# Padding scatters spread between the result scatters in a two-layer mixture-of-experts block with attention

## The chip, the cores and the metric

The kernel runs on one core of one Trainium2 chip. The metric is the device time of one execution in microseconds (us); less is better. A core has five engines that each take their own instruction stream in order and meet at semaphores: PE (TensorE, matmuls), DVE (VectorE), ACT (ScalarE), POOL (GpSimd, which here issues the indirect transfers) and SP (SyncE, which here issues the plain transfers).

## The reference

The block is x + FFN/2, then attention, then FFN/2 again, on 4 x 512 tokens of width 256. Only the FFN is touched. It is a mixture of 16 experts with the best 4 for each token:

```
t = xf * jax.lax.rsqrt(jnp.mean(xf * xf, axis=-1, keepdims=True) + EPS) * norm_w
logits = t @ gate_w.T + gate_b
vals, idx = jax.lax.top_k(logits, TOP_K)
gates_k = jax.nn.softmax(vals, axis=-1)
...
h = jnp.einsum('mh,eoh->emo', t, w1) + b1[:, None, :]
a = jnp.minimum(h[..., ::2], LIMIT)
b = jnp.clip(h[..., 1::2], -LIMIT, LIMIT)
act = a * jax.nn.sigmoid(ALPHA * a) * (b + 1.0)
y = jnp.einsum('emi,edi->emd', act, w2) + b2[:, None, :]
delta = jnp.einsum('me,emd->md', G, y)
```

## The kernel before

`moe(m)` is called twice, as m = 0 and m = 1, with `attention()` between. Each call has three stages.

**Routing.** The 2048 tokens are 16 tiles of 128, in four groups g of four tiles. For each group DVE centres the rows, PE turns them and multiplies them with the gate weights, DVE finds the four best experts (`choose`), PE counts by matmuls with a triangle of ones how many earlier tokens chose the same expert (`rank`), and DVE turns these ranks into row numbers (`locate`). Every expert owns a region of REGION rows in the DRAM tensor `x_rows`. POOL scatters the rows of each tile to their four experts, four indirect transfers to a tile, 64 in a stage. `slots()` on DVE then works out the table `slot_tab`: for each of 79 slots its first row in `x_rows`, the place of its goals and its expert. A slot is a tile of 128 rows of one expert, in the experts' order.

**Padding.** An expert's last tile is seldom full. POOL fills it by one scatter of `pad` for each expert, 16 in a stage, 128 rows each, from the row after its last token on. The goal number in a pad row is out of bounds, so that its result is dropped. Slot n < 16 belongs to an expert not above n, so SP waits before loading the rows of slot n for pads up to that of expert n. Before the change the pads count on five semaphores, for experts 0, 1, 2 to 3, 4 to 7 and 8 to 15 (`PADS`), and SP waits at slots 0, 1, 2, 4 and 8.

**Slots.** For n = 0 to 78 SP reads two numbers of slot n from `slot_tab` (`value_load`, two of them), issues the load of its rows and that of its goals into one of NX = 8 buffers (`load_rows`), PE turns the rows (`turn_rows`), ACT copies them to SBUF (`rows_out`), PE does the first product (`up`), ACT and DVE the gelu and the clipping, PE turns h (`turn_h`), does the second product (`down`), ACT copies y to SBUF (`y_out`), and POOL scatters y to the DRAM tensor `y_rows`. For n of 8 and more, SP's load waits until PE has turned slot n - 7 and until y of slot n - 8 is stored. PE goes in iterations s: up(s), turn_rows(s + 2), turn_h(s - 1), down(s - 2). ACT goes gelu(s), rows_out(s + 2), h_hi(s), y_out(s - 2). Neither has another order to fall back on: what stands behind a waiting instruction waits too.

At the end DVE adds the four results of each token (`combine`).

Of the kernel before, what the change touches and what calls it, by code (L numbers as in the profile page):

```python
# [19 lines left out]
ALU = mybir.AluOpType  # L20
# [25 lines left out]
def build(nc, x, wqkv, bias_qk, bv, wo, bo, query_rows, key_rows, norm_w, gate_w, gate_b, w1, b1, w2, b2, out):  # L46
# [56 lines left out]
    with ctx:  # L103
# [26 lines left out]
        def moe(m):  # L130
            with ExitStack() as own:
# [34 lines left out]
                pos = tmp("pos", [P, TPB, E])  # L166
                row_to = tmp("row_to", [P, NT, K], u32)
# [31 lines left out]
                PADS = (1, 2, 4, 8, 16)  # L199
                padded = [ev(f"padded{j}") for j in range(len(PADS))]  # L200
                pad_group = lambda e: next(j for j, last in enumerate(PADS) if e < last)

# [6 lines left out]
                with nc.Block() as block:  # L209
                    @block.sync  # L210
                    def _(sp):
# [6 lines left out]
                        def load_rows(n):  # L218
                            c = n % NX
                            row0 = sp.value_load(slot_tab[0:1, 0, n:n + 1], min_val=0, max_val=E * REGION + (E - 2) * P)  # L220
                            cell = sp.value_load(slot_tab[0:1, 1, n:n + 1], min_val=0,  # L221
                                                 max_val=(E * REGION + (E - 2) * P + 1) * ROW - 1)
                            if n >= NX:
                                sp.wait_ge(ev("turned"), n - NX + 1)
                                sp.wait_ge(y_stored[(n - NX) % NY], (n - NX) // NY * 16 + 16)
                            if n < E and n in (0,) + PADS:
                                sp.wait_ge(padded[pad_group(n)], 16 * (PADS[pad_group(n)] - n))
                            sp.dma_start(rows[:, c, :], x_rows[m].bitcast(f16)[bass.ds(row0, P), 0:2 * H]).then_inc(loaded[c], 16)
                            cells = x_rows[m].rearrange("r c -> (r c)")
                            sp.dma_start(goal[:, c, :], cells[bass.ds(cell, P * ROW)]  # L230
                                         .rearrange("(p c) -> p c", p=P)[:, 0:1],
                                         allow_slow_non_contiguous=True).then_inc(loaded[c], 16)
# [26 lines left out]
                        sp.wait_ge(ev("slot_tab"), 1)  # L259
                        sp.wait_ge(ev("idle_made"), 16)  # L260
                        for c in range(NR):
                            sp.wait_ge(scattered[c], NT // NR * K * 16)
                        for n in range(SLOTS):
                            load_rows(n)
# [14 lines left out]
                    def _(pool):  # L279
# [35 lines left out]
                        for e in range(E):  # L315
                            pool.indirect_dma_start(x_rows[m], bass.IndirectOffsetOnAxis(ap=pad_at[:, e:e + 1], axis=0),
                                                    pad[:, :], None).then_inc(padded[pad_group(e)], 16)
                        for n in range(SLOTS):
                            c = n % NX
                            pool.wait_ge(loaded[c], 32 * (n // NX) + 32)  # L320
                            pool.wait_ge(ev("y"), n + 1)
                            pool.indirect_dma_start(y_rows[m], bass.IndirectOffsetOnAxis(ap=goal[:, c, :], axis=0),  # L322
                                                    y[:, n % NY, :], None, bounds_check=K * T - 1, oob_is_err=False).then_inc(y_stored[n % NY], 16)

                    @block.tensor
                    def _(pe):
# [18 lines left out]
                        def rank(g):  # L345
# [6 lines left out]
                            for i in range(g * TPB):  # L352
                                pe.matmul(bank[4][:, 0:TPB * E].rearrange("p (t e) -> p t e", e=E), ones16[:, :],
                                          mask16[:, i:i + 1, :].broadcast_to([P, TPB, E]), start=False, stop=False,
                                          skip_group_check=True)
# [7 lines left out]
                            for t in range(TPB):  # L363
                                i = g * TPB + t
                                mm = pe.matmul(bank[5][:, 0:E], ones16[:, :], mask16[:, i, :], start=(i == 0),
                                               stop=(i == NT - 1), skip_group_check=True)
                            if g == B - 1:
                                mm.then_inc(ev("counts"), 1)
# [86 lines left out]
                    def _(act):  # L455
# [34 lines left out]
                        for g in range(B):  # L490
# [22 lines left out]
                            if m == 0:  # L513
                                for _ in range(SPLITS[g]):
                                    hi_split(split)
                                    split += 1
                        rows_out(0)
# [15 lines left out]
                    def _(dve):  # L533
# [87 lines left out]
                        def locate(g):  # L621
# [3 lines left out]
                                              region[:, :].unsqueeze(1).broadcast_to([P, TPB, E]), ALU.add)\  # L625
# [4 lines left out]
                            with nc.allow_low_precision("whole numbers"):  # L630
                                dve.tensor_reduce(row_to[:, some, :], work[:, :, :, :], AX.X, ALU.add)\  # L631
                                   .then_inc(ev("row_to"), 1)

# [9 lines left out]
                        def slots():  # L643
                            dve.wait_ge(ev("counts"), 1)
                            step(dve.tensor_scalar(count[:, :], bank[5][:, 0:E], P - 1.0, None, ALU.add))
                            dve.scalar_tensor_tensor(pad_at[:, :], bank[5][:, 0:E], place[:, 0:1], region[:, :],
                                                     ALU.add, ALU.add).then_inc(ev("pad_at"), 1)
# [72 lines left out]
                        if m == 0:  # L720
                            dve.wait_ge(ev("constants"), 9)
                        for g in range(B):
# [590 lines left out]
```

## Time and profile before

| what | value |
|---|---|
| median of 3 runs | 1123.13 us (1119.69 to 1123.15) |
| the profiled execution | 1121.11 us |
| its span | 1119.4 us |
| mean granted TensorE clock | 0.863 of full |
| PE busy | 737.8 us (66%) |
| DVE busy | 622.3 us (56%) |
| ACT busy | 425.2 us (38%) |
| POOL busy | 370.7 us (33%) |

The span is the time from the first to the last instruction; 1.7 us of the execution lie outside it. A busy share is an average over stages with different limits, so the stages are read apart. In what follows, m0 and m1 are the two calls, and all times without another word are from the start of the span.

### The profile page before, as it was taken

Reading aid. Unit: us, or ns where it says so; the run is one execution under the profiler, and the core shown is the slowest. Engines: PE = TensorE matmul, PEld = TensorE weight load, DVE = VectorE, ACT = ScalarE, POOL = GpSimd, SP = SyncE. Lnnn points to the kernel's source line nnn. Section 1 sums busy time; section 2 is a strip of 40 time slices with the busy share of each in tenths; the row PEclk is TensorE's granted clock in tenths of the full one; section 3 lists DMA queues with packets and bytes.
Section 4 is the critical chain, followed back from the end, with each engine's and each line's share of the span. In section 5 each row is a group of like instructions: output and inputs, shape, how many; then the busy total and the mean of one; then the engine's idle time right before and its main releaser. Section 6 shows DMA issues by size and latency. Waiting matters only on the chain. (4 is left out here: it accounts for less than half of the span.)

```text
span 1119.4 us, 22068 instructions
## 1 busy us (share of the span) xinstructions
PE 737.8 (66%) x5770; PEld 449.6 (40%) x5770; DVE 622.3 (56%) x1953; ACT 425.2 (38%) x945; POOL 370.7 (33%) x404
## 2 busy tenths in 40 slices
PE   2222169999999107658999998531205999999930
PEld 1112036666666003323343443421202666666620
DVE  6876036566665484446767672462502656665537
ACT  3433035555555012204545454110103555555510
POOL 4866723333333103440000000064772333333320
PEclk9999989999999657866999999755556999999975
DMA  9752323333332553420111100222232333333347
GB/s 321 253 211 94 118 75 91 87 96 89 91 88 83 188 169 95 131 76 16 45 31 35 33 27 3 76 87 72 98 113 72 92 93 96 94 93 92 83 146 230
DMA packets 110387, 114.31 MB, mean 102 GB/s; under 512 B 38836, under 2 KB 96669, under 8 KB 110272
## 3 DMA queue, kind: packets, MB, share of 16 engines
q1 hardware_dynamic: 95008, 73.82, 23.1%
q0 software_dynamic: 15264, 39.10, 9.4%
q8 instruction: 55, 0.90, 0.3%
q14 instruction: 60, 0.49, 0.1%
HBM read 60.89 MB, written 55.56 MB: 104 GB/s over the span
## 5 line engine op out<-in xcount | busy, mean ns | idle before, releaser
L322 POOL DMA_INDIRECT y_rows<-y_m,goal_m x158 | 155.6, 985 | 302.2 <-ACT y_m L486 282.9
L394 PE MATMUL banks<-w1s,rT_m 128*128 x948 | 234.6, 384 | 0.0
L671 DVE TENSOR_SCALAR b_m<-banks 128x256 f32<-128x256 f32 x158 | 67.1, 425 | 218.2 <-ACT p_m L472 110.3
L312 POOL DMA_INDIRECT x_rows<-row_m,row_to_m x128 | 135.0, 1054 | 121.2 <-DVE row_to_m L631 83.7
L1197 DVE CUSTOM_DVE_ANT_0 junk<-banks,maskq 128x128 bf16<-128x128 f32 (+3 forms) x256 | 115.6, 488 | 44.9 <-PE banks L1046 41.8
L465 ACT ACTIVATE rT_m<-banks 128x512 f16<-128x512 f16 x158 | 93.5, 592 | 105.4 <-issue 78.3
L394 PEld LDWEIGHTS banks<-w1s,rT_m 128*128 128x128 f16 x948 | 93.9, 99 | 97.5 <-issue 5.0
L416 PE MATMUL banks<-w2s,hT_m 128*128 x948 | 129.2, 273 | 0.0
L1166 ACT ACTIVATE probs<-banks 128x1024 f32<-128x1024 f32 (+3 forms) x128 | 86.1, 703 | 88.7 <-PE banks L1082 88.5
L376 PE MATMUL banks<-ident,rows_m 128*128 128x128 f16 x632 | 62.7, 223 | 79.2 <-DMA goal_m<-x_rows 40.0
L472 ACT ACTIVATE p_m<-banks 128x256 f32<-128x256 f32 x158 | 60.7, 384 | 116.7 <-PE banks L394 111.2
L376 PEld LDWEIGHTS banks<-ident,rows_m 128*128 128x128 f16 x632 | 48.9, 100 | 119.0 <-DMA goal_m<-x_rows 43.1
L416 PEld LDWEIGHTS banks<-w2s,hT_m 128*128 128x128 f16 x948 | 92.6, 98 | 8.9
L479 ACT ACTIVATE hs_m<-h_m 128x256 f16<-128x256 f32 x158 | 65.8, 417 | 73.8 <-DVE h_m L679 45.1
L1046 PE MATMUL banks<-k_stack,q_stack 63*128 63x128 f16 (+3 forms) x256 | 72.0, 327 | 21.9 <-DVE mx L1197 9.7
L686 DVE TENSOR_TENSOR hs_m<-h_m,hs_m 128x256 f16<-128x256 f32 x158 | 67.2, 426 | 30.6 <-ACT hs_m L479 7.8
L332 PE MATMUL banks<-ident,u_m 128*128 128x128 f32 x64 | 19.8, 436 | 82.3 <-DVE u_m L576 52.9
L679 DVE SCALAR_TENSOR_TENSOR h_m<-p_m,b_m 128x256 f32<-128x256 f32 x158 | 67.1, 425 | 5.4
L709 DVE SCALAR_TENSOR_TENSOR X<-arena_m,gate_m,X 128x256 f32<-128x256 f32 x128 | 51.4, 477 | 31.3 <-DMA arena_m<-y_rows 30.9
L1002 POOL COPY v_near<-v 128x272 f32<-128x272 f32 x16 | 6.6, 416 | 182.7 <-PE banks L1095 182.7
L693 DVE COPY hT_m<-banks 128x512 f16<-128x512 f16 x158 | 65.8, 416 | 1.0 <-PE banks L403 1.0
L403 PE MATMUL banks<-ident,hs_m 128*128 128x128 f16 x632 | 61.3, 220 | 4.1 <-DVE hs_m L686 2.6
(165 smaller groups left out, 1160.4 us busy)
## 6 DMA issues: line engine op xcount, KB each, us to landing
rows_m<-x_rows SPq DMA_DIRECT2D x158, 128.0 KB
arena_m<-y_rows SPq DMA_DIRECT2D x32, 512.0 KB, 5.4
arena_m<-in_w SPq DMA_DIRECT2D x16, 512.0 KB, 7.4
arena_m<-in_w SPq DMA_DIRECT2D x16, 256.0 KB, 8.4
qk_split<-w_raw SPq DMA_DIRECT2D x32, 128.0 KB
x_rows<-pad SPq DMA_DIRECT2D x2, 2040.0 KB, 9.9
q_stack<-qk_split SPq DMA_DIRECT2D x32, 96.0 KB
k_stack<-qk_split SPq DMA_DIRECT2D x32, 96.0 KB
```

The source lines that it names most:

```text
L312: pool.indirect_dma_start(x_rows[m], bass.IndirectOffsetOnAxis(ap=row_to[:, i, k:k + 1], axis=0), row[:, i % NR, :], None).then_inc(scatte ...
L322: pool.indirect_dma_start(y_rows[m], bass.IndirectOffsetOnAxis(ap=goal[:, c, :], axis=0), y[:, n % NY, :], None, bounds_check=K * T - 1, o ...
L376: mm = pe.transpose(bank16[n % 2][:, q * P:(q + 1) * P], rows[:, c, q * P:(q + 1) * P], ident16[:, :])
L394: mm = pe.matmul(o, rT[:, n % 2, 2 * r + k, :], w1s[:, bass.ds(e, 1), k, w, :], start=False, stop=(k == HC - 1 and w == 1))
L416: mm = pe.matmul(o, hT[:, n % 2, 2 * r + k, :], w2s[:, bass.ds(e, 1), k, w, :], start=False, stop=(k == 1 and w == 1))
L465: act.activation(rT[:, n % 2], bank16[n % 2][:, 0:512].rearrange("p (q n) -> p q n", q=4), ACT.Copy).then_inc(ev("rT"), 1)
L671: dve.tensor_scalar(b[:, n % 2, :], bank[2 + n % 2][:, INNER:], (LIMIT + 1.0) * S, (1.0 - LIMIT) * S, ALU.min, ALU.max).then_inc(ev("b"), 1)
L679: dve.scalar_tensor_tensor(h[:, n % 2, :], p[:, n % 2, :], GELU_LIMIT, b[:, n % 2, :], ALU.min, ALU.mult).then_inc(ev("h"), 1)
L686: dve.tensor_tensor(hs[:, n % 2, 2:4, :], h[:, n % 2, :].rearrange("p (k n) -> p k n", k=2), hs[:, n % 2, 0:2, :], ALU.subtract).then_inc( ...
L1046: pe.matmul(bank[u % 2][:, 0:(i + 1) * P], stacks[0][at:at + HALF - 1, pair, i * P:(i + 1) * P], stacks[1][at:at + HALF - 1, pair, 0:(i + ...
L1166: act.activation(probs[j][:, 2 * pl:2 * pl + 2, :], banks[:, first:first + 2, 0:SEQ - j * P], ACT.Exp, scale=0.25).then_inc(s("exp"), 1)
L1197: dve.tensor_tensor_reduce(junk[:, (n * U + u) % 3, 0:W], bank[u % 2][:, 0:W], maskq[:, SEQ - W:], 1.0, -3e38, ALU.add, ALU.max, mx[:, n % ...
```

## The change

The diff, cut to its core:

```
-                PADS = (1, 2, 4, 8, 16)
-                padded = [ev(f"padded{j}") for j in range(len(PADS))]
-                pad_group = lambda e: next(j for j, last in enumerate(PADS) if e < last)
+                padded = [ev(f"padded{e}") for e in range(E)]
+                AHEAD = 6
...
-                        def load_rows(n):
-                            c = n % NX
+                        def place_of(n):
                             row0 = sp.value_load(slot_tab[0:1, 0, n:n + 1], ...)
                             cell = sp.value_load(slot_tab[0:1, 1, n:n + 1], ...)
+                            return row0, cell
+
+                        def load_rows(n, row0, cell):
+                            c = n % NX
...
-                            if n < E and n in (0,) + PADS:
-                                sp.wait_ge(padded[pad_group(n)], 16 * (PADS[pad_group(n)] - n))
+                            if n < E:
+                                sp.wait_ge(padded[n], 16)
...
                         sp.wait_ge(ev("slot_tab"), 1)
+                        places = [place_of(n) for n in range(4)]
                         sp.wait_ge(ev("idle_made"), 16)
...
                         for n in range(SLOTS):
-                            load_rows(n)
+                            load_rows(n, *(places[n] if n < 4 else place_of(n)))
...
-                        for e in range(E):
+                        def pad_expert(e):
                             pool.indirect_dma_start(x_rows[m], ... pad_at[:, e:e + 1] ...,
-                                                    pad[:, :], None).then_inc(padded[pad_group(e)], 16)
+                                                    pad[:, :], None).then_inc(padded[e], 16)
+
+                        for e in range(AHEAD):
+                            pad_expert(e)
                         for n in range(SLOTS):
                             c = n % NX
+                            if 1 <= n and n - 1 + AHEAD < E:
+                                pad_expert(n - 1 + AHEAD)
                             pool.wait_ge(loaded[c], 32 * (n // NX) + 32)
                             pool.wait_ge(ev("y"), n + 1)
...
-                            for i in range(g * TPB):
-                                pe.matmul(bank[4][:, 0:TPB * E]..., ones16[:, :], mask16[:, i:i + 1, :]...)
...
-                                mm = pe.matmul(bank[5][:, 0:E], ones16[:, :], mask16[:, i, :], start=(i == 0), ...)
-                            if g == B - 1:
-                                mm.then_inc(ev("counts"), 1)
+                                mm = pe.matmul(bank[5][:, g * E:(g + 1) * E], ones16[:, :], mask16[:, i, :], start=(t == 0), ...)
+                            mm.then_inc(ev("counts"), 1)
...
+                        act.preload_act_table_set("gelu_apprx_sigmoid_and_others")
                         rows_out(0)
...
-                                              region[:, :].unsqueeze(1).broadcast_to([P, TPB, E]), ALU.add)\
+                                              base[:, g, :].unsqueeze(1).broadcast_to([P, TPB, E]), ALU.add)\
...
+                            dve.wait_ge(ev("counts"), g + 1)
+                            step(dve.tensor_tensor(base[:, g + 1, :], base[:, g, :], bank[5][:, g * E:(g + 1) * E], ALU.add))
```

Four things change. (1) Only the pads of experts 0 to 5 follow the row scatters; that of expert n + 5 now stands just ahead of the scatter of y of slot n, for n = 1 to 10, and every one of slots 0 to 15 has a wait for its own pad. (2) SP reads the places of slots 0 to 3 before it waits for the row scatters. (3) `rank` no longer multiplies the masks of all earlier groups; DVE carries the totals in `base` and adds the group's counts after each group. (4) ACT loads the table of the gelu before rows_out(0), not at the first gelu.

POOL's instructions at the end of routing in m0, before (what an instruction waits for stands in brackets; `y_0` is the semaphore of y_out in m0):

```order
L312 DMA x_rows<-row_m,row_to_m 36992x272 [waits row_to_0,row_hi_0]
L312 DMA x_rows<-row_m,row_to_m 36992x272 x3
L316 DMA x_rows<-pad,pad_at_m 36992x272 [waits pad_at_0]
L316 DMA x_rows<-pad,pad_at_m 36992x272 x15
L322 DMA y_rows<-y_m,goal_m 8192x256 [waits y_0,rows_loaded0_0]
L322 DMA y_rows<-y_m,goal_m 8192x256 [waits y_0,rows_loaded1_0]
```

and of the changed kernel at the same place, L320 the pads and L331 the scatters of y:

```order
L316 DMA x_rows<-row_m,row_to_m 36992x272 x3
L320 DMA x_rows<-pad,pad_at_m 36992x272 [waits pad_at_0]
L320 DMA x_rows<-pad,pad_at_m 36992x272 x5
L331 DMA y_rows<-y_m,goal_m 8192x256 [waits y_0,rows_loaded0_0]
L320 DMA x_rows<-pad,pad_at_m 36992x272
L331 DMA y_rows<-y_m,goal_m 8192x256 [waits y_0,rows_loaded1_0]
```

Ten pads have moved behind a scatter that waits for y, the pad of expert 6 behind that of slot 0, and so on one by one.

SP's instructions for slot 2 in m0, before:

```order
L220 TENSOR_LOAD slot_tab_m
L220 ISA x2
L221 TENSOR_LOAD slot_tab_m
L221 ISA x2
L228 ISA [waits padded2_0]
L228 DMA rows_m<-x_rows 128x512
L230 REGISTER_ALU
L230 DMA goal_m<-x_rows 128x1
```

and of the changed kernel, for slot 2, slot 3 and slot 6's wait:

```order
L231 ISA [waits padded2_0]
L231 DMA rows_m<-x_rows 128x512
L233 REGISTER_ALU
L233 DMA goal_m<-x_rows 128x1
L231 ISA [waits padded3_0]
L231 DMA rows_m<-x_rows 128x512
L233 REGISTER_ALU
L233 DMA goal_m<-x_rows 128x1
...
L231 ISA [waits padded6_0]
```

The reads of the table are gone from between the first four loads, and slots 3, 5, 6 and so on, which had no wait for a pad, have one.

## Rows read from the trace of the kernel before

**Rows 1.** Busy time by stretch: start:end, length, busy of each engine, PEclk, DMA.

```profile
125.00:154.00 29.00, 8.06 (x29) 3.40 (x30) 1.27 (x3) 3.81 (x7) 14.71 (x16) 0.84 0.31 100
826.00:857.00 31.00, 4.49 (x20) 2.29 (x21) 0.00 (x0) 2.73 (x4) 15.66 (x17) 0.50 0.26 90
857.00:1075.00 218.00, 214.83 (x1721) 141.83 (x1718) 132.55 (x332) 123.06 (x314) 75.81 (x77) 1.00 0.31 86
```

**Rows 2.** Timeline, end of routing in m0: start, length, engine, line, operation.

```profile
137.15 0.61 PE L376 MATMUL banks<-ident,rows_m 128*128 128x128 f16 x4 [6.29 <-issue]
...
143.31 0.97 POOL L316 DMA_INDIRECT x_rows<-pad,pad_at_m  x1 [0.30 <-issue]
...
147.85 0.00 SPq L228 DMA_DIRECT2D rows_m<-x_rows  x1
...
149.88 0.61 PE L376 MATMUL banks<-ident,rows_m 128*128 128x128 f16 x4 [9.14 <-DMA goal_m<-x_rows]
```

**Rows 3.** Timeline of POOL in m1: the first and the last pad.

```profile
826.42 0.97 POOL L316 DMA_INDIRECT x_rows<-pad,pad_at_m  x1 [0.30 <-issue]
...
845.57 0.97 POOL L316 DMA_INDIRECT x_rows<-pad,pad_at_m  x1 [0.30 <-issue]
```

**Rows 4.** Chain of waits in m1, from the last row scatter to slot 1.

```profile
827.67 0.70 SPq L220
...
833.03 0.70 SPq L228
...
851.23 0.00 SPq L228
...
851.93 1.14 DMA goal_m<-x_rows
```

**Rows 5.** Timeline in m1: turns of slots 1, 4, 6; scatters of y 0 to 2.

```profile
853.12 0.61 PE L376 MATMUL banks<-ident,rows_m 128*128 128x128 f16 x4 [13.55 <-DMA goal_m<-x_rows]
...
860.95 0.39 PE L376 MATMUL banks<-ident,rows_m 128*128 128x128 f16 x4
...
866.69 0.39 PE L376 MATMUL banks<-ident,rows_m 128*128 128x128 f16 x4
...
864.04 1.00 POOL L322 DMA_INDIRECT y_rows<-y_m,goal_m  x1 [17.50 <-ACT y_m L486]
867.04 0.99 POOL L322 DMA_INDIRECT y_rows<-y_m,goal_m  x1 [2.01 <-ACT y_m L486]
869.75 0.98 POOL L322 DMA_INDIRECT y_rows<-y_m,goal_m  x1 [1.71 <-ACT y_m L486]
```

**Rows 6.** Chain of waits: transfers that ended a wait, from their issue to landing.

```profile
804.73 2.45 DMA x_rows<-row_m,row_to_m
...
896.96 4.12 DMA y_rows<-y_m,goal_m
...
909.16 4.10 DMA goal_m<-x_rows
...
1076.52 2.11 DMA y_rows<-y_m,goal_m
```

**Rows 7.** Timeline of ACT in m1: h_hi in a steady iteration.

```profile
868.22 0.42 ACT L479 ACTIVATE hs_m<-h_m 128x256 f16<-128x256 f32 x1 [0.46 <-issue]
```

**Rows 8.** Timeline of PE in m1: the first product of slot 0 and of slot 3.

```profile
853.95 2.77 PE L394 MATMUL banks<-w1s,rT_m 128*128 x6
...
862.67 1.46 PE L394 MATMUL banks<-w1s,rT_m 128*128 x6
```

**Rows 9.** Timeline of ACT in m1: table load and first gelu.

```profile
854.38 1.28 ACT L472 ACT_TABLE_LOAD   x1
...
856.75 0.39 ACT L472 ACTIVATE p_m<-banks 128x256 f32<-128x256 f32 x1 [1.09 <-PE banks L394]
```

**Rows 10.** Timeline in m0, group 3: ranks, row numbers, the scatters behind them.

```profile
94.78 0.83 PE L353 MATMUL banks<-mask_m,ones 128*128 128x64 f16 x12
...
99.99 0.22 DVE L624 TENSOR_TENSOR pos_m<-banks,region 128x64 f32<-128x64 f32 x1 [5.16 <-remote]
...
101.91 0.97 POOL L312 DMA_INDIRECT x_rows<-row_m,row_to_m  x1 [3.94 <-DVE row_to_m L631]
```

More of the change, by code:

```diff
@@ L166, in moe @@
                 pos = tmp("pos", [P, TPB, E])
+                base = tmp("base", [P, B + 1, E])
                 row_to = tmp("row_to", [P, NT, K], u32)
@@ L351, in rank @@
                                       skip_group_check=True)
-                            for i in range(g * TPB):
-                                pe.matmul(bank[4][:, 0:TPB * E].rearrange("p (t e) -> p t e", e=E), ones16[:, :],
-                                          mask16[:, i:i + 1, :].broadcast_to([P, TPB, E]), start=False, stop=False,
-                                          skip_group_check=True)
                             for t in range(TPB - 1):
@@ L364, in rank @@
                                 i = g * TPB + t
-                                mm = pe.matmul(bank[5][:, 0:E], ones16[:, :], mask16[:, i, :], start=(i == 0),
-                                               stop=(i == NT - 1), skip_group_check=True)
-                            if g == B - 1:
-                                mm.then_inc(ev("counts"), 1)
+                                mm = pe.matmul(bank[5][:, g * E:(g + 1) * E], ones16[:, :], mask16[:, i, :], start=(t == 0),
+                                               stop=(t == TPB - 1), skip_group_check=True)
+                            mm.then_inc(ev("counts"), 1)
                         def turn_rows(n):
@@ L643, in slots @@
                         def slots():
[L644 to L647, printed above, removed]
+                            step(dve.scalar_tensor_tensor(count[:, :], base[:, B, :], P - 1.0, region[:, :],
+                                                          ALU.add, ALU.subtract))
+                            dve.tensor_scalar(pad_at[:, :], base[:, B, :], place[:, 0:1], None, ALU.add)\
+                               .then_inc(ev("pad_at"), 1)
                             step(dve.tensor_scalar(count[:, :], count[:, :], 7, None, ALU.arith_shift_right))
@@ L721, in _ @@
                             dve.wait_ge(ev("constants"), 9)
+                        step(dve.tensor_copy(base[:, 0, :], region[:, :]))
                         for g in range(B):
```

## The prediction, made before the changed kernel ran

> **What bounds the kernel now.** I read the table of stages first. The slot stages are near full use of PE: 214.83 us busy in 218 us, at the full clock of 2.4 GHz. Between routing and slots there is a hole: from 826 to 857 us PE works 4.49 us, in m0 from 125 to 154 us 8.06 us, while POOL is busy half the time [rows 1]. The change works on these two holes and on the first slots behind them.
>
> The timelines show what fills the holes. POOL's pads run without a pause, 0.97 us and a gap of 0.30 us each, so one every 1.28 us, from 826.42 to 846.5 us in m1 [rows 3] and up to 144.3 us in m0 [rows 2]. They are not what SP waits for: a row scatter takes 2.45 us from its issue to landing [rows 6], so the pad of expert 1, which slot 1 needs, lands at about 830.2 us. The chain of waits shows SP itself crawling, its register steps and reads of the table in steps of 0.70 us, from 827.67 to 851.23 us [rows 4]. It gets fast 4.7 us after POOL's last pad has ended. In m0 the load of slot 2 goes out at 147.85 us, 3.6 us after the last pad [rows 2]. So in both calls a long unbroken run of POOL's scatters goes with a slow SP, which recovers about 4 us after the run. What the one does to the other the trace doesn't say. I take the end of the run as what sets the end of the hole.
>
> **What the change takes away.** Ten pads leave the run: 10 x 1.28 = 12.8 us. SP then gets fast at about 851.2 - 12.8 = 838.4 us in m1. PE turned slot 1 1.9 us after SP's load of it (851.23 to 853.12 us, [rows 4, 5]), so now at about 840.4 us. The early reads help to have this: in the slow stretch reading the table for slot 0 took from 827.67 to 833.03 us, 5.4 us [rows 4], and for slots 1 to 3 the reads are now done while the last row scatters run. Slots 0 and 1 are thus loaded by the time that SP is fast, and the gain in m1 is the whole 12.7 us. In m0 slot 1 was turned already at 137.15 us, and what came late was slot 2, at 149.88 us [rows 2]. Here SP gets fast at 135.1 us, slot 2 follows at about 138, behind slot 1 and the first product: a gain near 12 us. Sum of both: **24.5 us**. The bounds are 20 us (SP recovers some 2 us later in each call than I take) and 36.5 us (the slow stretch is gone: slot 1 in m1 at 830.2 + 2.3 = 832.5, 20.5 us early, and slot 2 in m0 at 134, 16 us early).
>
> **What the change puts on the path.** The pad of expert n, for n = 6 to 15, is issued behind the scatter of y of slot n - 6, and SP waits for it before it loads slot n. In the trace of before, y of slot 0 is scattered at 864.04 us and PE turns slot 6 at 866.69 us, 2.65 us later [rows 5]; for slot 7 it is 867.04 and 866.69 + 2.72 = 869.41, so 2.37 us. (2.72 us is the period of a slot: the scatters of y at 867.04 and 869.75 us stand 2.71 us apart.) All of this would be moved early together. In that distance the changed kernel must fit a path L of three terms:
>
> - The pad is issued 1.28 us behind the scatter of y [rows 3].
> - It lands: 2.45 us for a row scatter of the same size, 2.11 us for the last scatter of y, alone, and 4.12 us for one amid the slots' traffic [rows 6]. I take 2.8 us, nearer to the lone ones, since POOL and SP now take turns.
> - SP issues the load of rows and goals, and they land: 1.9 us from the load to PE's turn in m1, 2.0 us in m0 [rows 2, 4, 5], and 4.1 us for the goals alone amid traffic [rows 6]. I take 2.7 us, because the next scatter of y and its pad fall into this load.
>
> L = 1.28 + 2.8 + 2.7 = 6.8 us; at the least 1.28 + 2.11 + 1.9 = 5.3, at the most 1.28 + 4.12 + 4.2 = 9.6 us. Even the least is twice the 2.65 us that are there, so PE waits.
>
> It waits again and again, because the loop closes on itself. Behind PE's turn of slot n stands, in PE's order, down(n - 4), and behind ACT's copy of slot n stand h_hi and y_out of the same iteration. The turn of slot 4 at 860.95 and y of slot 0 at 864.04 are 3.09 us apart [rows 5]. In a stall h is ready before, so that ACT's idle 0.46 us ahead of h_hi falls away [rows 7], and 2.6 us are left. So slot n + 2 can be turned no sooner than 2.6 + L after slot n, where before two slots took 5.44 us. With L = 6.8 that is 9.4 us for two slots. Slots 6 to 15 are five pairs. The first loses L - 2.37, the others L + 2.6 - 5.44 = L - 2.84 each: 5 L - 13.7 in all, **20.3 us** in a call and **40.6 us** in both. The bounds are 12.8 and 34.3 us in a call. From slot 16 on there is no pad to wait for. Scatters of y are then eight slots ahead of the loads as before, and PE takes up its period at once. What was lost isn't given back, since PE has next to nothing free there [rows 1].
>
> The waits for pads 0 to 5 cost nothing: they are issued by 834 us, in the stretch in which SP is slow anyway.
>
> **Ranks.** PE drops 4, 8 and 12 matmuls in groups 1 to 3; twelve take 0.83 us. In m0, group 3, the path from ranks to POOL is bare: POOL stands idle 3.94 us for row_to, and DVE before it 5.16 us for the ranks [rows 10]. I take group 2, with eight matmuls, to be alike. DVE gains one small addition a group (0.22 us, as that of L624), behind row_to, and once the wait for `counts`. I count a gain of 0.6 + 0.8 - 0.4 = **1 us** in m0 and none in m1, where POOL has 16 scatters of the group before to go through. If DVE's 5.16 us were the matmuls themselves, up to 6 us could come back, if the extra waits were slow in the slow stretch as SP's steps were, 2 us lost.
>
> **Table of the gelu.** The load takes 1.28 us from 854.38 us, and the first gelu starts at 856.75, just when the product that it waits for ends (853.95 + 2.77 = 856.72) [rows 8, 9]. It is hidden by the product, so moving it early brings nothing. Without that cover it would cost the 1.28 us. The Trainium skill ("ScalarE: Activation LUTs", What ACT_TABLE_LOAD costs) has about 2.66 us for a switch, a drain of 1.38 us included; were this on the path, the sum would be 5.3 us lower. The row shows it under the product, and I keep zero.
>
> **Sum.** 1121.1 (the profiled execution) - 24.5 + 40.6 - 1 = 1136.2 us. The profiled execution is 2.0 us under the median of the three runs, so I put the forecast at **1137 us**, 14 us or 1.2% slower.
>
> **The rivals.**
> *The burst wins (faster).* The same two terms, the other way: if the slow stretch vanishes with the shorter run (36.5 us gained) and L is near its least, 5.4 us (13.3 us lost in a call), the result is 1121.1 - 36.5 + 26.6 - 1 = 1110 us. It turns at 5 L - 13.7 = 12.3 us in a call, L = 5.2 us, with the gain that I take, and at L = 6.4 us with the full gain. For it speaks that SP's slowness has no cause in its own work, and that row scatters also run ahead of it, at the same pace; against it that these, 16 to a group, stay in the run, and SP was slow at 827.67 us, before a second pad could matter.
>
> *A wash.* The two terms within 3 us of each other, for instance L = 5.8 us with a gain of 30: 1121.1 - 30 + 30.6 - 1, so 1121 us. It is what is left between.
>
> *The clock falls in the stalls.* PE would stand still some 4 us of each 9.4. Over the hole of m0 the granted clock is 0.84 on the mean, so it fell to the lower level while PE stood idle, and in that of m1 it stood at 0.50 throughout [rows 1]: six matmuls of the first product took 2.77 us at 1.2 GHz and 1.46 us at 2.4 GHz [rows 8]. If it falls in the stalls, turn_h and the second product between a turn and y take about 1 us longer, once for each pair, in 10 pairs: 10 us, and 1147 us. The Trainium skill ("TensorE: Matmul & The Clock Gate", Part 1) has the clock set by how busy PE has lately been, which speaks for it; at 60% busy in the stalled slots I think it mostly holds.
>
> *The waits don't bind*, because the pads come in time: excluded by the 2.65 us of [rows 5], which are less than the landing of one transfer and its load.
>
> **Chances and range.** My forecast 0.60 (its own range 1126 to 1150 us), the clock's fall on top 0.14, a wash 0.11, the burst wins 0.15. The range of 8 in 10 goes from 1116 to 1160 us: the lower end takes in the wash, the upper one L = 8.5 us or the clock with L = 7.5 us. A difference under 0.3% (3.4 us) is no change for this measurement. Faster 0.15, same 0.11, slower 0.74.
>
> **What would show it.** In the changed profile the last of the six pads starts at about 7.7 us behind the last row scatter, in both calls. SP's first four loads stand close together, and slot 1 is turned some 12 us sooner after the last row scatter in m1. From slot 6 to 15 PE's turns wait for loads of goals or rows, in pairs 9 to 10 us apart, and the chain of waits runs over y, POOL, x_rows, goal and PE; from slot 16 the period is 2.72 us. ACT's table load stands before the first rT. I am wrong if pads land so fast that the pairs are under 8 us apart, if SP is quick at once, or if SP stays slow through the new pattern of two scatters for a slot.

## The result, and the profile after

The changed kernel takes **1149.56 us** (median of 4 runs, 1147.31 to 1151.09), the kernel before in the same rounds 1123.14 us (1119.69 to 1124.46). The ratio is 1.0231, its 95% interval 1.0199 to 1.0263: 26 us slower, where 14 were forecast. The time lies in the range of 1116 to 1160 us, and at the upper edge of the forecast's own range. The profiled execution has a span of 1145.6 us against 1119.4.

The page of the changed kernel, its busy time and the group of PE's turns of the rows (a turn is the transposition of a slot's rows by PE, `turn_rows`):

```profile
PE 752.8 (66%) x5722; PEld 451.5 (39%) x5722; DVE 624.8 (55%) x1963; ACT 426.1 (37%) x945; POOL 368.4 (32%) x404
...
L380 PE MATMUL banks<-ident,rows_m 128*128 128x128 f16 x632 | 63.6, 225 | 72.4 <-DMA goal_m<-x_rows 72.4
```

Nearly all of PE's idle time ahead of its turns is put down to loads of goals. PE does fewer matmuls than before and is busy longer, which points to a lower clock. The table of stages tells where (start:end, length, busy of PE, its weight loads, DVE, ACT and POOL, then clock, DMA share and GB/s):

```profile
125.00:154.00 29.00, 17.35 (x104) 9.59 (x105) 7.71 (x19) 8.67 (x20) 6.86 (x7) 0.97 0.26 75
144.00:196.00 52.00, 35.73 (x217) 20.17 (x215) 16.09 (x40) 16.02 (x40) 20.05 (x20) 0.84 0.25 76
...
836.00:865.00 29.00, 11.66 (x69) 6.33 (x70) 4.49 (x11) 5.54 (x13) 7.04 (x9) 0.61 0.22 67
865.00:916.00 51.00, 36.02 (x222) 19.78 (x219) 16.93 (x42) 16.61 (x42) 20.58 (x21) 0.87 0.26 81
916.00:1100.00 184.00, 181.70 (x1451) 120.36 (x1451) 111.18 (x279) 102.48 (x263) 64.93 (x66) 0.99 0.31 86
```

The holes of [rows 1] are partly filled: from 125 to 154 us PE is busy 17.35 us, where it was busy 8.06. Behind them stands what was not there before, some 50 us in each call in which PE is busy 70% of the time, at a granted clock of 0.84 and 0.87. Behind slot 16 PE is as busy as before: 181.70 us of 184 from 916 us on, where [rows 1] have 214.83 of 218.

The timeline of m0 shows one round of the new stall and the last of the six pads (start, length, engine, line, operation, and in brackets the idle time ahead and what ended it):

```profile
127.67 0.97 POOL L320 DMA_INDIRECT x_rows<-pad,pad_at_m  x1 [0.30 <-issue]
...
144.38 0.99 POOL L331 DMA_INDIRECT y_rows<-y_m,goal_m  x1 [15.73 <-ACT y_m L490]
145.68 0.99 POOL L320 DMA_INDIRECT x_rows<-pad,pad_at_m  x1 [0.30 <-issue]
148.32 0.33 SPq L231 DMA_DIRECT2D rows_m<-x_rows  x1
150.69 0.40 PE L380 MATMUL banks<-ident,rows_m 128*128 128x128 f16 x4 [3.49 <-DMA goal_m<-x_rows]
...
153.04 2.75 PE L398 MATMUL banks<-w1s,rT_m 128*128 x6
154.09 1.00 POOL L331 DMA_INDIRECT y_rows<-y_m,goal_m  x1 [4.43 <-ACT y_m L490]
155.40 0.98 POOL L320 DMA_INDIRECT x_rows<-pad,pad_at_m  x1 [0.30 <-issue]
155.60 0.41 PE L380 MATMUL banks<-ident,rows_m 128*128 128x128 f16 x4
```

Y of slot 0 goes out at 144.38, the pad of expert 6 at 145.68, SP's load of slot 6 at 148.32, and PE turns it at 150.69 us: 6.31 us, the forecast's L. The turn of slot 7, at 155.60 us, has no idle time ahead: it stands right behind the first product of slot 5, which began at 153.04 us and took 2.75 us. The chain of waits in m1 shows a whole turn of the loop (start, length, what):

```profile
869.21 1.78 DMA goal_m<-x_rows
870.99 0.05 issue
871.04 0.40 PE banks L380 x4
871.43 0.36 issue
871.79 0.38 PE banks L407 x4
872.18 0.11 PE banks L416
872.28 1.02 PE banks L420 x6
873.31 0.02 issue
873.33 0.39 ACT y_m L490
...
873.84 0.73 issue
874.57 0.99 POOL y_rows L331
875.56 0.30 issue
875.87 2.69 DMA x_rows<-pad,pad_at_m
...
878.77 0.33 SPq L231
...
879.28 1.44 DMA goal_m<-x_rows
880.72 0.33 issue
881.05 0.40 PE banks L380 x4
```

From turn to y 3.53 us, from y to the turn two slots on 6.48 us, together 10.0 us for two slots, which took 5.44 before [rows 5]. What SP waited for from 864 to 916 us (us in all, times, the longest) is nearly all pads:

```profile
SPq L230 <- DMA x_rows<-pad,pad_at_m: 24.1, 8, 4.9
```

**Where the 26.2 us went.** I cut each call at the last row scatter and at PE's turns of slots 5 and 15.

| stretch | before m0, m1 | after m0, m1 | change |
|---|---|---|---|
| start to last row scatter, m0 | 122.90 | 120.03 | -2.9 |
| last row scatter to turn of slot 5 | 36.1, 38.8 | 24.3, 28.4 | -22.2 |
| turn of slot 5 to turn of slot 15 | 27.2, 27.2 | 53.4, 50.8 | +49.8 |
| all the rest | | | +1.5 |

Of the rest, 2.2 us lie at slot 16 of m1, which is turned 4.94 us after slot 15 and not 2.72, behind a first product of 2.53 us. The next turn comes 2.72 us later.

### The profile page after: what moved, and what is told of

The parts are those of the page before. It is cut to its first block and busy times, and to the rows that moved or that the text cites. A ratio compares the mean times of both kernels' runs of the same rounds, so it can differ in the third digit from the quotient of the medians.

```text
span 1145.6 us, 21990 instructions
## 1 busy us (share of the span) xinstructions
PE 752.8 (66%) x5722; PEld 451.5 (39%) x5722; DVE 624.8 (55%) x1963; ACT 426.1 (37%) x945; POOL 368.4 (32%) x404
## 3 DMA queue, kind: packets, MB, share of 16 engines
q1 hardware_dynamic: 95008, 73.82, 22.5%
## 5 line engine op out<-in xcount | busy, mean ns | idle before, releaser
L331 POOL DMA_INDIRECT y_rows<-y_m,goal_m x158 | 155.7, 985 | 329.4 <-ACT y_m L490 305.6
L398 PE MATMUL banks<-w1s,rT_m 128*128 x948 | 243.2, 395 | 0.0
L316 POOL DMA_INDIRECT x_rows<-row_m,row_to_m x128 | 132.1, 1032 | 121.6 <-DVE row_to_m L636 84.1
L1205 DVE CUSTOM_DVE_ANT_0 junk<-banks,maskq 128x128 bf16<-128x128 f32 (+3 forms) x256 | 115.6, 488 | 44.7 <-PE banks L1054 41.7
L398 PEld LDWEIGHTS banks<-w1s,rT_m 128*128 128x128 f16 x948 | 96.2, 101 | 104.1 <-issue 16.0
L420 PE MATMUL banks<-w2s,hT_m 128*128 x948 | 133.0, 278 | 0.0
L407 PE MATMUL banks<-ident,hs_m 128*128 128x128 f16 x632 | 61.5, 220 | 8.0 <-issue 4.9
```

The costliest lines, as they stand in the source:

```text
L398: mm = pe.matmul(o, rT[:, n % 2, 2 * r + k, :], w1s[:, bass.ds(e, 1), k, w, :], start=False, stop=(k == HC - 1 and w == 1))
L407: mm = pe.transpose(bank16[4 + n % 2][:, q * P:(q + 1) * P], hs[:, n % 2, q, :], ident16[:, :])
L420: mm = pe.matmul(o, hT[:, n % 2, 2 * r + k, :], w2s[:, bass.ds(e, 1), k, w, :], start=False, stop=(k == 1 and w == 1))
L1205: dve.tensor_tensor_reduce(junk[:, (n * U + u) % 3, 0:W], bank[u % 2][:, 0:W], maskq[:, SEQ - W:], 1.0, -3e38, ALU.add, ALU.max, mx[:, n % ...
```

## The experiments

Their ratios stand against the kernel before in the same rounds; its median moved from 1120.61 to 1124.56 us between the sets of rounds, so where two experiments come from different sets I compare ratios. In the diffs, lines with - are the changed kernel's. Times "after the last row scatter" run from its start to PE's turn of a slot, m0 and m1.

### How many pads go first

`e1_all_pads_first`: the change without its new order, all 16 pads behind the row scatters.

```
-                AHEAD = 6
+                AHEAD = 16
```

> The changed kernel with AHEAD = 16, so that all pads follow the row scatters again; ranks, early reads, table and one semaphore for each pad stay. Theory W (SP's waits for pads issued behind y cost 24 us in m0 and 26 us in m1, the shorter run of scatters gives 10.4 us in each call back): 1149.6 - 49.8 + 20.8 = 1120.6 us, 2.5 us under the kernel before, all of it from routing in m0. Rival T (the waits of SP for one pad each, or the other three edits, cost the time): near 1149 us.

`e2_ahead_10`, `e3_ahead_8` and later `e10_ahead_7`: the same line with 10, 8 and 7.

> AHEAD = 10: six pads go behind scatters of y, but each ten slots ahead. Between the scatter of y of slot n - 10 and the turn of slot n lie 2.65 + 4 x 2.72 = 13.5 us, twice the path L of 6.3 to 6.8 us. Theory W: no stall, and six pads at 1.04 us each less in the run: 1120.6 - 12.5 = 1108 us. Rival T (two scatters in a slot's time crowd POOL or the DMA engines): six slots a call with 2.5 us lost each, so 1108 + 30 = 1138 us.

> AHEAD = 8: eight pads go behind scatters of y, each eight slots ahead: 2.65 + 2 x 2.72 = 8.1 us are there, L was 6.3 to 6.8 us. Theory W: it just fits, and the run is eight pads shorter: 1120.6 - 16.6 = 1104 us, the fastest. If L is over 8.1 us amid full traffic (4.1 us for landing and 3.5 us for the load were seen there), stalls of 1 us for a slot come back and it ends near 1115 us. Rival T: near 1144 us.

> The changed kernel with AHEAD = 7. The loop then closes over three slots: the turn of slot n + 3 comes no sooner than 3.4 + L = 9.8 us after that of slot n (L = 6.4 as measured with AHEAD = 6), where three slots take 8.16 us: 0.55 us a slot for nine slots, 5 to 6 us a call, against 24 to 26 with AHEAD = 6. By that the time lies halfway between AHEAD = 6 (1149.6) and 8 (1117.4), but nearer to 8: 1117.4 + 11 + 2 = 1130 us. If the loss were by traffic of pad and y together, one place more would change nothing: 1148 us.

| pads first | median us | ratio, interval | slot 2, us after last row scatter | slot 5 to slot 15, us | SP's waits for pads there, us |
|---|---|---|---|---|---|
| 6 (the change) | 1149.56 | 1.0231, 1.0199 to 1.0263 | 16.6, 20.9 | 53.4, 50.8 | 26.0, 25.0 |
| 7 | 1122.39 | 0.9988, 0.9958 to 1.0018 | 22.4, 22.5 | 38.1, 37.0 | 8.6, 7.1 |
| 8 | 1117.39 | 0.9934, 0.9901 to 0.9967 | 23.1, 23.5 | 33.8, 34.5 | 2.3, 2.8 |
| 10 | 1116.82 | 0.9950, 0.9923 to 0.9978 | 25.6, 26.0 | 30.5, 32.9 | none |
| 16 | 1125.61 | 1.0007, 0.9981 to 1.0033 | 33.2, 34.4 | 27.2, 27.2 | none |

(Pairs are m0 and m1. The fifth column runs from PE's turn of slot 5 to that of slot 15, as in the table of the stretches.)

With 16 first the loss is gone, so it belongs to the moved pads. From 16 to 10 and 8 slot 2 comes 8 to 11 us sooner in each call, where 1.28 us a pad would give 7.7 and 10.2; from 16 to 6 it comes 16.6 and 13.5 us sooner, for 12.8. So the shorter run does what was forecast of it; at 10 and 8 it wins.

Between 7 and 6 lie 27 us. The loop takes 10.0 us, from the turn of slot n over y of slot n - 4 and its pad to the turn of slot n + 2 with 6 pads first, of n + 3 with 7, of n + 4 with 8, and two, three and four slots have 5.4, 8.2 and 10.9 us at their period of 2.72: a deficit of 4.6, of 1.8 and none. I expected 1130 us of 7 and got 1122.39: the direction held, the size not.

That is not all that the moved pads cost. From slot 5 to slot 15 the deficit of 1.8 us in three slots makes 6 us in a call, and the turns lose 10.9 and 9.8; with 8 pads first it makes nothing, and they lose 6.6 and 7.3; with 10, 3.2 and 5.7. At 10 SP waits for no pad in that stretch, so this isn't the loop of the pads. It is most of why 10 and 8 missed what was expected of them without a stall, 1108 and 1104 us; the rest came with e1, itself 5 us over its 1120.6, for which see the early reads. What SP waits for there is the landing of y (of slot n - 8 before it loads slot n), with 10 pads first in m1:

```profile
SPq L230 <- DMA y_rows<-y_m,goal_m: 8.1, 4, 3.1
```

With 16 first it waits for the same, but 4.5 us in six times, and the turns keep their pace. The likely cause is the one that e4 shows below: a scatter between two scatters of y costs time by itself. By which way these waits reach PE no run separates. The scan has its flat bottom from 8 to 10.

### The pads alone, and the table alone

`e9_pads_alone`: the kernel before, with the new order of the pads (AHEAD = 6) and their 16 semaphores and nothing else of the change.

```
 (the kernel before)
+                        for e in range(AHEAD):
+                            pad_expert(e)
                         for n in range(SLOTS):
+                            if 1 <= n and n - 1 + AHEAD < E:
+                                pad_expert(n - 1 + AHEAD)
```

> The kernel before with the pads' edit alone: AHEAD = 6, a semaphore for each pad, the pads of experts 6 to 15 behind scatters of y. If the pads carry the whole loss: the changed kernel's 1149.6 us, plus 3 us for the ranks that are missing, minus 2 to 4 us for the early reads that are missing: 1147 to 1151 us. If the other edits share in it: nearer to 1140 us.

1151.62 us (1145.05 to 1155.31), ratio 1.0230 (1.0180 to 1.0280). The pads alone carry the whole loss. Its trace has the same parts: slot 5 to slot 15 takes 51.3 and 53.5 us, 50.4 us more than before in both calls, and slot 5 is turned 24.7 and 27.8 us after the last row scatter. The rest of the change as made adds up to nothing that this measures, to within some 5 us; it may hold a gain and a loss that cancel.

`e8_table_alone`: the kernel before with the one line that loads the gelu's table early.

```
+                        act.preload_act_table_set("gelu_apprx_sigmoid_and_others")
                         rows_out(0)
```

> The kernel before with only the table of the gelu loaded ahead of rows_out(0). If the load is hidden by the first product, as the profile showed: 1124 us, no change (within 0.2%). If it was on the path, by its 1.28 us in both calls, 2.6 us (0.23%) less, by the skill's 2.66 us a switch 5.3 us less.

1122.32 us, ratio 1.0007 (0.9986 to 1.0028): no change. In the changed kernel the load stands in ACT's idle time (timeline of ACT, m0):

```profile
99.85 1.28 ACT L521 ACT_TABLE_LOAD   x1
```

### Is it the waiting or the traffic?

`e4_spare_scatters`: as e1, with a scatter of `pad` to a tensor that nobody reads ahead of the scatters of y of slots 1 to 10, where the change has its pads. Nothing waits for them but the end of the call; the extra tensor, its indices and these twenty scatters are added work.

```
-                AHEAD = 6
+                AHEAD = 16
...
-                            if 1 <= n and n - 1 + AHEAD < E:
-                                pad_expert(n - 1 + AHEAD)
+                            if 1 <= n <= 10:
+                                pool.indirect_dma_start(spare_rows[m], ..., pad[:, :], None).then_inc(ev("spare_done"), 16)
```

> All 16 pads follow the row scatters as in the kernel before; and in the places of the ten moved pads POOL issues ten scatters of the same size and data to a spare tensor that nobody reads, so the output is whole and only work is added. It has the traffic and POOL's order of the changed kernel without SP's wait. Theory W: as with all pads first, 1120.6 us, at most 3 us more. Rival T (traffic, POOL's time): 1120.6 + 49.8 = 1170 us.

1136.96 us, ratio 1.0111 (1.0077 to 1.0144), 11.4 us over e1 in the same rounds. The turns keep their 2.7 us up to slot 7; then PE stalls in places, from slots 8 and 9 on, the first whose loads wait for y of eight slots before. From slot 5 to slot 15 SP's waits for such landings come to 7.5 and 10.2 us, where e1 has 6.7 and 4.5. From the turn of slot 2 to that of slot 15 it takes 41.7 and 44.5 us in m0 and m1, where e1 has 34.2 and 34.9: 17 us more, some 7 us of it made up by a shorter hole in this profiled execution. So 128 more rows to scatter between two y are not free, 0.57 us each by the times and 0.86 by these turns. I had put them at nothing, at most 3 us. This bounds the traffic's part in the change from above only loosely, since here they are extra work, while the change moves its pads.

### The early reads

`e5_all_first_late_reads` is e1, `e6_ahead_8_late_reads` is e3, both with the places of slots 0 to 3 read as before the change, each ahead of its own load.

```
-                        places = [place_of(n) for n in range(4)]
...
-                            load_rows(n, *(places[n] if n < 4 else place_of(n)))
+                            load_rows(n, *place_of(n))
```

> All pads first (AHEAD = 16) and the places of slots 0 to 3 read at their slots as in the kernel before; of the change only the ranks on carried totals, the early table and one semaphore a pad are left. Theory R (the early reads cost time in the slow stretch: SP must step through eight reads at 0.7 us a step before it issues slot 0's load): slot 2 is turned 27 and 31 us after the last row scatter as before, against 33.2 and 34.4 us with the early reads, and the time is 1125.6 - 7 = 1118 us, 0.2 to 0.5% under the kernel before by the earlier routing. Rival (early reads do no harm): 1125 us.

> AHEAD = 8 with late reads. Theory R: slot 0 is turned in the slow stretch, 14 us after the last row scatter, slot 1 some 2 us after SP gets fast, so about 2 us earlier in each call than with early reads: 1117.4 - 4 = 1113 us. Rival (early reads help, since SP has less to do once it is fast): 1120 us.

e5: 1117.39 us, ratio 0.9969 (0.9950 to 0.9988), where e1 has 1.0007. e6: 1111.62 us, 0.9920 (0.9890 to 0.9950), where e3 has 0.9934. By the ratios the late reads are better by 4 us with all 16 pads first, just clear of the uncertainty, and by 1.6 us with 8, which is within it. The traces show the mechanism. SP and PE in m0, of e1 (timeline, one fence), from the last pad on:

```profile
140.45 0.97 POOL L320 DMA_INDIRECT x_rows<-pad,pad_at_m  x1 [0.30 <-issue]
...
146.66 0.36 SPq L231 DMA_DIRECT2D rows_m<-x_rows  x1
...
149.06 0.61 PE L380 MATMUL banks<-ident,rows_m 128*128 128x128 f16 x4 [30.87 <-DMA goal_m<-x_rows]
```

and of e5, timeline of the same place:

```profile
126.92 0.71 SPq L231 DMA_DIRECT2D rows_m<-x_rows  x1
...
130.27 0.61 PE L379 MATMUL banks<-ident,rows_m 128*128 128x128 f16 x4 [14.39 <-issue]
...
139.07 0.97 POOL L319 DMA_INDIRECT x_rows<-pad,pad_at_m  x1 [0.30 <-issue]
```

With two reads ahead of it the first load goes out at 126.92 us, amid the run, and slot 0 is turned 11.6 us after the last row scatter, where it is 29.0 with eight. By slot 5 only 2.8 us are left of that lead. The eight reads do crawl under the run, as the chain of waits of the changed kernel shows in m1:

```profile
845.23 0.69 SPq L220
...
848.73 0.69 SPq L220
...
850.41 0.36 SPq L231
```

There slot 0 is turned 16.5 us after the last row scatter, at 852.81 us, where it was 13.8 us before the change. It is not so in every call: in m0 of the changed kernel and of e4, which has e1's early reads and its 16 pads, the first load goes out at 128.00 and 130.48 us. Whether the eight reads are done before the slow stretch begins seems to decide it. With six pads first the reads made no difference that the traces show: e9, which reads late, has slot 5 at 24.7 and 27.8 us after the last row scatter, the changed kernel at 24.3 and 28.4.

### Breaking the run of scatters

`e7_gate`: late reads, six pads, then POOL waits for the rows of slot 3 to be loaded, then four more pads, and the other six one by one as in e2.

```
-                AHEAD = 6
+                AHEAD = 10
...
-                        for e in range(AHEAD):
+                        for e in range(6):
+                            pad_expert(e)
+                        pool.wait_ge(loaded[3], 32)
+                        for e in range(6, AHEAD):
                             pad_expert(e)
```

> Six pads follow the row scatters, then POOL waits until slot 3's rows are loaded, then pads 6 to 9 follow, and from there AHEAD = 10; late reads. Theory S (SP is slow because POOL's scatters run without a pause, and gets fast 4 to 5 us after a pause begins): SP gets fast as in the changed kernel, slot 2 is turned 17 to 21 us after the last row scatter instead of 26, pads 6 to 9 land well before slot 6: 1116.8 - 10 = 1107 us. Rival (SP's slowness depends on the number of pads or on time since the table was made): no gain over AHEAD = 10, 1117 us. Pad 6 is issued at slot 3's load, 3 slots or 8 us ahead of the turn of slot 6; if that is too late, 2 us are lost in each call.

1106.80 us (1105.30 to 1108.33), ratio 0.9869 (0.9841 to 0.9897): the lowest median of this study, 14 us under before. Its timeline in m0:

```profile
126.61 0.97 POOL L319 DMA_INDIRECT x_rows<-pad,pad_at_m  x1 [0.30 <-issue]
...
126.68 0.70 SPq L231 DMA_DIRECT2D rows_m<-x_rows  x1
131.33 0.33 SPq L231 DMA_DIRECT2D rows_m<-x_rows  x1
...
138.70 0.97 POOL L319 DMA_INDIRECT x_rows<-pad,pad_at_m  x1 [11.13 <-DMA goal_m<-x_rows]
```

SP's load takes 0.70 us while POOL scatters and 0.33 us 3.8 us after the sixth pad has ended (127.58). Slot 2 is turned 17.8 and 20.0 us after the last row scatter, as in the changed kernel, and pads 6 to 9 are there early enough: slot 15 comes after 57.7 and 61.5 us, where the changed kernel needs 77.7 and 79.2. Against e2 this kernel has two things changed, the gate and the late reads. The nearest kernel without the gate is e6 of the same rounds, late reads and 8 pads first: 1111.62 us, none of its runs (from 1110.20) as low as the highest of this one (1108.33). So the gate is worth some 5 us over the best kernel without it; 10 pads first with late reads and no gate was not run.

`e11_gate_after_4`: the same with the gate behind four pads, at the rows of slot 1.

```
-                        for e in range(6):
+                        for e in range(4):
                             pad_expert(e)
-                        pool.wait_ge(loaded[3], 32)
-                        for e in range(6, AHEAD):
+                        pool.wait_ge(loaded[1], 32)
+                        for e in range(4, AHEAD):
```

> As the kernel with the gate (1106.8 us), but only four pads follow the row scatters, POOL then waits for slot 1's rows, and pads 4 to 9 follow. Theory S: the first run is 2.6 us shorter in each call and SP gets fast that much sooner: 1106.8 - 5 = 1102 us. The second run of six pads is 7.7 us; if it makes SP slow again while slots 2 to 5 are loaded, the gain is lost or turned round: 1107 us or more.

1107.44 us (1102.46 to 1113.31), ratio 0.9856 (0.9806 to 0.9906), the same as e7. Slot 2 comes 2.5 and 2.2 us sooner still, after 15.3 and 17.8 us, and the six pads behind the gate take it back, so that the 1102 us of a shorter first run did not come. Timeline in m0:

```profile
132.99 0.97 POOL L319 DMA_INDIRECT x_rows<-pad,pad_at_m  x1 [6.12 <-DMA goal_m<-x_rows]
...
135.85 0.33 SPq L233 DMA_DIRECT2D goal_m<-x_rows  x1
...
139.39 0.70 SPq L231 DMA_DIRECT2D rows_m<-x_rows  x1
141.52 0.01 SPq L233 DMA_DIRECT2D goal_m<-x_rows  x1
```

SP's step is 0.33 us at 135.85 and 0.70 us again at 139.39, 6.4 us into the second run of pads, and the load of the goals follows 2.1 us behind that of the rows, as in the slow stretch. Slot 5 is turned after 26.3 us in m0, where e7 has 24.9.

## Why the prediction was right or wrong, point by point

The forecast's own change was +15.1 us of the profiled execution, and the spans differ by 26.2. The 11.1 us between them are 9.2 of the loop, 2.3 of the holes and 1.5 of the rest, less 1.9 that routing in m0 was shorter than forecast. (1136.2 us and the 2.0 us that the profiled execution lies under the median make 1138 and not 1137 us.)

**The loop of pads: right in kind, 9 us too small.** Two slots take 10.7 us in m0 and 10.2 in m1 from slot 5 to slot 15, and behind them the period of 2.72 us is back (turns at 200.41 and 203.13 us). e9 shows that these pads alone make the whole loss, e1 that it is gone with them. The odd slots from 5 to 15 form a chain without a gap, from each turn to the y of four slots before and from that to the turn of two slots on. Five distances from turn to y, and five from y to turn, which is L:

| | forecast, each call | m0 | m1 |
|---|---|---|---|
| turn to y, each | 3.07, then 2.6 | 3.07, 3.10, 4.26, 3.22, 3.11 | 3.07, 3.07, 3.41, 3.12, 3.82 |
| sum | 13.5 | 16.8 | 16.5 |
| L, each | 6.8 | 8.21, 7.79, 6.25, 6.67, 7.69 | 8.20, 6.82, 6.57, 6.51, 6.21 |
| sum | 34.0 | 36.6 | 34.3 |

The term that was mis-sized most is "2.6 us are left" from a turn to y: 6.3 of the 9.2 us by which 49.8 exceeds 40.6. No turn of this stretch has its y sooner than 3.07 us, the distance of the steady state, so ACT's idle 0.46 us did not fall away; that is 3.8 us in eight distances. The other 2.5 us are restarts. Most of it stands in the two longest distances, 4.26 and 3.82 us: turn_h begins up to 0.4 us after the turn has ended, and the second product takes 1.48 and 1.46 us where it takes 0.82 in the steady state (timeline), at a granted clock of 0.50 (166.50 to 169.60 us) and 0.52 (906.50 to 908.00 us). L makes the other 2.9 us. The rounds shown above are among its shorter ones, 6.31 and 6.48 us: issue 1.3, from the pad to the load of the rows 2.6 and 2.9 (2.8 taken for the landing), load to turn 2.4 and 2.3 (2.7 taken). The longest stand at slot 7 in both calls, 8.2 us, and there PE did not wait for the load: the turn stands behind a first product of 2.75 and 2.62 us, where the steady state has 1.46.

**The clock: a rival that came partly true.** It was given as another way, with 10 us on top. PE's rows in the first restart of m0 (windows, columns as above):

```profile
150.60:154.00 3.40, 2.95 (x19) 1.79 (x20) 0.76 (x2) 1.28 (x3) 0.00 (x0) 0.74 0.16 39
154.00:155.50 1.50, 1.50 (x5) 0.48 (x4) 0.00 (x0) 0.00 (x0) 1.10 (x2) 0.50 0.00 0
```

PE had stood idle 3.49 us, and the granted clock is 0.74 and then 0.50, which is 1.2 GHz; the first product at 153.04 us takes 2.75 us, as it did in [rows 8] at that clock. "At 60% busy in the stalled slots I think it mostly holds" was wrong: it fell in stalls, though not through all of them (0.84 on the mean). What the engine did before the fall agrees with the Trainium skill ("TensorE: Matmul & The Clock Gate", Part 1), by which the clock follows how busy PE has lately been. How much of the 9 us is the clock and how much the restart itself no run separates. An estimate from rows: the 2.5 us of the restarts between turn and y and the 1.4 us by which L exceeds 6.8 at slot 7 of each call stand beside such slow products, some 5 us of the 9.2.

**The traffic of the moved pads: not in the sum.** e4 shows that such scatters between y cost time by themselves, 0.57 us each by their times. In the changed kernel it lies inside the measured distances. In the two rounds shown, landing and load were not longer than forecast; slot 9 of m0 was turned 3.84 us after its load went out (162.65 to 166.49 us), for 2.7 taken. With 8 and 10 pads first, where the loop hardly binds, it is the likely cause of what is left of the loss.

**The gain in the holes: right in kind, 22.2 us for 24.5.** The last of six pads starts 7.64 us behind the last row scatter in m0 and 7.66 in m1, as forecast. By slot 5 m0 has gained 11.8 us, for 12 forecast, and m1 10.4, for 12.7. SP gets fast 5.2 us after POOL's run in m1 (844.93 to 850.12), where 4.7 was taken, and slot 1 is turned 17.5 us after the last row scatter, for 15.3 forecast. "Slots 0 and 1 are thus loaded by the time that SP is fast" did not happen: the first load of m1 goes out at 850.41 us. "The early reads help to have this" was wrong as well: in m1 they put the load of slot 0 behind eight slow reads in place of two, and it comes later. But this isn't what the missing 2.3 us are made of, since e9 without the early reads has the same gain, 22.5 us; there slot 1 is turned 17.0 us after the last row scatter, its own reads still to come when SP gets fast. With all 16 pads first the early reads do cost time (e1 against e5).

**Ranks: 2.9 us in these two traces, where 1 was taken.** DVE's wait in group 3 [rows 10] fell from 5.16 to 0.19 us (timeline of DVE, m0):

```profile
96.06 0.22 DVE L629 TENSOR_TENSOR pos_m<-banks,base_m 128x64 f32<-128x64 f32 x1 [0.19 <-issue]
...
102.50 0.17 DVE L639 TENSOR_TENSOR base_m<-base_m,banks 128x16 f32<-128x16 f32 x1 [5.30 <-issue]
```

The wait has moved to the new addition, behind row_to and off POOL's path. How much that is worth the traces don't fix. The last row scatter of m0 starts at 122.90, 121.23 and 128.77 us in the three traces without the new ranks (before, e8, e9) and at 118.63 to 121.73 us in the ten with them, so 2.9 us is within what one kernel and the next differ by. By the times, e5 is the nearest to the ranks alone (with them only the table, which does nothing, and one semaphore for each pad): ratio 0.9969, 1 to 6 us gained, between the 1 us taken and the 6 named as the upper bound. In m1 nothing came of it, as forecast (93.56 us from first to last row scatter before, 93.70 after).

**The table: hidden, as forecast.** e8 shows it. The 2.66 us that the Trainium skill ("ScalarE: Activation LUTs", What ACT_TABLE_LOAD costs) gives for a switch would have been 5.3 us in two calls; the run shows none of it, since [rows 8, 9] had it under a product.

**The burst wins, and the wash,** have fallen for six pads: L was 6.9 us on the mean of the 20 slots, and the slow stretch did not vanish. With 8 pads first the time does fall, 7 us under before in e3, by way of a longer lead and not of a quick SP. That the time came inside the forecast's own range owes something to its width, 24 us.

**What stays open** is why SP crawls while POOL issues scatters back to back. In e7 it ended 3.8 us after a pause of POOL began, and in e11 a second run brought it back within 6.4 us; what of POOL's run does it (its instruction stream, descriptors or packets) no run separates. Open too is how a scatter between two y stalls PE. e6 against e3 is too near to its uncertainty to size the reads at eight pads.

## What to carry to other kernels

A transfer that stands in order behind work of the pipeline's own output must be ahead of its reader by more slots than the loop takes: add issue, landing, load, and the way from the reader back to that output, and divide by the period. Here 10 us by 2.72 is 3.7 slots, and the pads had two; the lead of 7 and 8 bought back what the loop took, until the longer run cost as much. Take the way back whole, with the order of the instructions on each engine and at the speed of a restart, and take nothing off for idle time in it that no trace shows to go. Scatters put between the result scatters cost something even where nothing waits for them. And if one engine slows while another issues a long run, a wait that breaks the run at the point where the first data are in can be worth more than a shorter run, while work moved early into the slow stretch delays what stands behind it.

## What the runs showed of the hardware that I had not expected

- SP's steps of 0.70 us come and go with POOL's unbroken runs of scatters: in e7 back to 0.33 us at 131.33, 3.8 us after a run, in e11 back to 0.70 us 6.4 us into a second one.
- One pad more ahead, 7 for 6, was worth 27 us: 1122.39 against 1149.56 us.
- From the same reads and 16 pads first, the first load of m0 went out 26.6 us after the last row scatter in e1 and 8.8 us after it in e4 (146.66 and 130.48 us).
- Twenty scatters of 128 rows that nothing in the slots waits for cost 11.4 us (e4). With 10 pads first and no wait for a pad, ten slots still took 3.2 and 5.7 us more than with 16 (e2 and e1).
- The granted clock didn't follow the length of the stall just before: after 1.61 us of idle time (turn at 900.58 us, changed kernel, m1) the second product ran at 1.00 and took 0.82 us, after 1.43 us (turn at 905.47 us) it ran at 0.52 and took 1.46 us.
